# Block positions from a row's first edge and one count, instead of fifty counts over all edges

## What is computed

```python
h = relu(layernorm(x)); x = x + attention_layer(h, node_type, src, dst)   # L0
h = relu(layernorm(x)); x = x + degree_normalised_sum(h, src, dst)        # L1
h = relu(layernorm(x)); x = x + gated_sum(h, edge_attr, src, dst)         # L2
h = relu(layernorm(x)); x = x + mean_layer(h, src, dst)                   # L3
# each: out[n] = sum over the edges e with dst[e] == n of f(h[src[e]], ...)
```

## Time and profile before

| | us |
|---|---|
| median of 3 runs | 5079.63 (5073.73 to 5083.69) |
| the profiled execution | 5077.58 |
| its span | 5075.4 |
| busy: POOL / VectorE / TensorE / ScalarE | 3396.0 / 3117.0 / 3020.8 / 1527.4 |
| mean granted TensorE clock | 0.717 of full |

### The profile page before, as it was taken

How to read it: one execution, slowest core, us unless ns; L and a number is a source line. 1 busy time by engine, 2 the same in 40 slices (tenths; PEclk the granted TensorE clock), 3 DMA queues, 4 the chain that set the end, 5 groups by cost and what they waited for, 6 DMA issues and landing times.

```text
span 5075.4 us, 78070 instructions
## 1 busy us (share of the span) xinstructions
PE 3020.8 (60%) x15683; PEld 2534.0 (50%) x15684; DVE 3117.0 (61%) x8273; ACT 1527.4 (30%) x2888; POOL 3396.0 (67%) x3564
## 2 busy tenths in 40 slices
PE   1846555555563444455555999999996444444443
PEld 1535455545553444444443777777775343434433
DVE  6467777777788666645553677777775344444443
ACT  3223333333313000001111666666664122222222
POOL 1277777777600777777774777777774777777775
PEclk9957777877777555557776999999998555555555
DMA  2367877877831222222224767767776222222224
GB/s 51 83 178 215 231 230 225 225 227 226 215 92 34 53 53 52 53 59 66 65 66 49 197 186 188 186 185 189 186 186 118 53 56 56 56 56 55 56 56 41
DMA packets 536532, 616.06 MB, mean 121 GB/s; under 512 B 98004, under 2 KB 420607, under 8 KB 536352
## 3 DMA queue, kind: packets, MB, share of 16 engines
q0 software_dynamic: 142176, 349.02, 27.2%
q1 hardware_dynamic: 394176, 265.13, 19.5%
HBM read 529.54 MB, written 84.25 MB: 121 GB/s over the span
## 4 chain that ended last, share of the span: by engine, by line
POOL 43%; issue 20%; DMA 14%; DVE 10%; PE 7%; DVEq 2%; ACT 2%; SPq 1%; POOLq 0%; ACTq 0%
POOL G L658 43%; DMA G<-tab,SRC 9%; DMA mvd<-G 3%; DVE ACCR L1384 3%; PE PB L493 2%; PE PSA L876 2%; PE PB L1066 1%; DVEq L617 1%; DMA MV<-mvd 1%; DVE ACCR L1856 1%; PE PB L486 1%; PE PB L1004 0%; DVE FLG L1838 0%; PE PB L1058 0%; ACT PB L1230 0%
## 5 line engine op out<-in xcount | busy, mean ns | idle before, releaser
L658 POOL DMA_INDIRECT G<-tab,SRC x3520 | 3358.2, 954 | 1432.9 <-issue 1044.5
L1384 DVE TENSOR_TENSOR ACCR<-ACCR,PSA 128x128 f32 (+2 forms) x3536 | 1127.7, 319 | 748.8 <-PE PSA L876 389.8
L876 PE MATMUL PSA<-G,S 128*128 128x128 f32 x3520 | 857.3, 420 | 1157.7 <-DMA G<-tab,SRC 975.8
L876 PEld LDWEIGHTS PSA<-G,S 128*128 128x128 f32 x3520 | 736.0, 309 | 1267.9 <-DVE ACCR L1384 690.9
L1367 DVE TENSOR_TENSOR S<-PB,REL 128x512 f32<-128x512 f32 x884 | 606.3, 686 | 38.9 <-DVE MASK L1436 13.7
L1004 PE MATMUL PB<-QTR,ST 128*128 x1792 | 339.8, 350 | 301.4 <-ACT ST L1193 147.4
L1004 PEld LDWEIGHTS PB<-QTR,ST 128*128 128x128 f32 x1792 | 299.9, 253 | 336.1 <-issue 335.7
L876 PE MATMUL PSA<-FLG,S 128*128 128x256 f32 x1760 | 427.2, 387 | 2.8 <-DVE FLG L1838 2.6
L876 PEld LDWEIGHTS PSA<-FLG,S 128*128 128x128 f32 x1760 | 340.5, 194 | 149.3 <-issue 88.3
L876 PE MATMUL PSA<-SCR,S 128*128 128x137 f32 x1792 | 332.0, 343 | 17.8 <-DVE ACCR L1384 17.6
L876 PEld LDWEIGHTS PSA<-SCR,S 128*128 128x128 f32 x1792 | 307.9, 249 | 22.8 <-DVE SCR L1747 22.8
(11 more groups left out here) (313 smaller groups left out, 3748.1 us busy)
## 6 DMA issues: line engine op xcount, KB each, us to landing
mvd<-G SPq DMA_DIRECT2D x224, 256.0 KB
MV<-mvd SPq DMA_DIRECT2D x224, 256.0 KB
G<-tab,SRC POOLq DMA_INDIRECT x3520, 2.5
SCR<-in_ea_t SPq DMA_DIRECT2D x880, 64.0 KB
S<-relt SPq DMA_DIRECT2D x224, 128.0 KB, 4.9
SCR<-reld SPq DMA_DIRECT2D x220, 128.0 KB
tab<-SCR SPq DMA_DIRECT2D x57, 128.0 KB, 1.8
tab<-G SPq DMA_DIRECT2D x50, 128.0 KB, 1.7
```

Of the source, the lines that this page charges most:

```text
L658: nc.gpsimd.indirect_dma_start(out=rows[:, slot, j, :], out_offset=None, in_=table, in_offset=bass.IndirectOffsetOnAxis(ap=SRC[:, k:k + 1] ...
L876: last = nc.tensor.matmul((PSA if banks is None else banks)[:, par, j, 0:width], S[:, slot, j, :], rhs(j), start=True, stop=True)
L1384: v_.tensor_tensor(rows, rows, banks[:, par, j, 0:width], ALU.add).then_inc(s["rows_added"], 1)
```

## The change

The 50 counts over all edges go, on VectorE and on ScalarE, with their thresholds. In their place each of 128 partitions finds the position for its own threshold, 128p (only those of partitions 0 to 49 are used):

1. SyncE loads the first edge's destination of each of the 128 rows, one word each, instead of the array.
2. VectorE puts these 128 words on a diagonal, TensorE spreads them to all partitions with a matmul of ones, and VectorE counts on partition p how many are under 128p. That number less one (not below 0) is the only row in which the stretch can begin.
3. POOL fetches that row for each partition with one indirect transfer: 128 rows of 831 words.
4. VectorE makes one count over 831 columns, adds 831 times the row number, puts the 50 results on a diagonal, and the same matmul as before (L956 there) brings them to all partitions.

```diff
+            pool.wait_ge(row_known, 1)
+            nc.gpsimd.indirect_dma_start(
+                out=DSTI, out_offset=None, in_=a["dst_pm"],
+                in_offset=bass.IndirectOffsetOnAxis(ap=row_i[:, 0:1], axis=0)).then_inc(dst_loaded, 16)
...
-            sp.dma_start(DSTI, a["dst_pm"]).then_inc(dst_loaded, 16)
+            with nc.allow_non_contiguous_dma(reason="a column"):
+                sp.dma_start(FIRSTI, a["dst_pm"][:, 0:1]).then_inc(firsts_loaded, 16)
...
-            pe.wait_ge(counted, half + 1)
-            pe.wait_ge(counted_too, NE - half)
+            pe.wait_ge(firsts_put, 1)
+            nc.tensor.matmul(FIRSTP, ones, FIRSTD, start=True, stop=True).then_inc(firsts_spread, 1)
+            pe.wait_ge(counted, 1)
             nc.tensor.matmul(PB[0][:, 0:NE], ones, cnt, start=True, stop=True).then_inc(reckoned, 1)
...
-            act.wait_ge(counted, 1)
-            def count(b):
-                nc.scalar.activation(JUNKA, DSTF, ACT.Sign, bias=thr_half[:, bass.ds(b, 1)], scale=-1.0,
-                                     accum_out=cnt[:, bass.ds(b, 1)]).then_inc(counted_too, 1)
-            count(half)
-            with act.Fori(half + 1, NE) as b:
-                act.wait_ge(counted_too, b - half)
-                count(b)
...
-            c(v_.tensor_copy(thr, thrI))
-            c(v_.tensor_scalar(thr_half, thr, -0.5, None, ALU.add))
...
-            c(v_.memset(cnt, 0.0))
+            c(v_.tensor_scalar(edge_f, minus_p, -float(P), None, ALU.mult))
             c(v_.memset(cum, 0.0))
+
+            dve.wait_ge(firsts_loaded, 16)
+            c(v_.tensor_copy(count_f, FIRSTI))
+            v_.tensor_scalar(FIRSTD, ident[:, :], count_f, None, ALU.mult).then_inc(firsts_put, 1)
+            dve.wait_ge(firsts_spread, 1)
+            c(v_.tensor_scalar(JUNK[:, 0:P], FIRSTP, edge_f, 0.0, ALU.is_lt, ALU.add, accum_out=row_f))
+            c(v_.tensor_scalar(row_f, row_f, -1.0, 0.0, ALU.add, ALU.max))
+            c(v_.tensor_copy(row_i, row_f))
+            dve.sem_inc(row_known, 1)
+
             dve.wait_ge(dst_loaded, 16)
-            v_.tensor_copy(DSTF, DSTI).then_inc(counted, 1)
-            with dve.Fori(0, half) as b:
-                dve.wait_ge(counted, b + 1)
-                v_.tensor_scalar(JUNK, DSTF, thr[:, bass.ds(b, 1)], 0.0, ALU.is_lt, ALU.add,
-                                 accum_out=cnt[:, bass.ds(b, 1)]).then_inc(counted, 1)
+            c(v_.tensor_copy(DSTF, DSTI))
+            c(v_.tensor_scalar(JUNK, DSTF, edge_f, 0.0, ALU.is_lt, ALU.add, accum_out=count_f))
+            c(v_.scalar_tensor_tensor(count_f, row_f, float(TC), count_f, ALU.mult, ALU.add))
+            v_.tensor_scalar(cnt, ident[:, 0:NE], count_f, None, ALU.mult).then_inc(counted, 1)
             dve.wait_ge(reckoned, TOTALS)
-            c(v_.tensor_copy(bf[:, 0:half], PB[0][:, 0:half]))
-
-            c(v_.tensor_scalar(bf[:, half:NE], PB[0][:, half:NE], 0.5, float(P * TC) / 2, ALU.mult, ALU.add))
+            c(v_.tensor_copy(bf, PB[0][:, 0:NE]))
```

More of the change, by code:

```diff
@@ L340, in build @@
         c_ready = sem("consts_ready")
-        dst_loaded = sem("dst_loaded")
+        firsts_loaded = sem("first_edges_loaded")
+        firsts_put, firsts_spread = sem("first_edges_put"), sem("first_edges_spread")
+        row_known = sem("boundary_row_known")
+        dst_loaded = sem("boundary_row_loaded")
         x_loaded = sem("x_loaded")
@@ L344, in build @@
         counted = sem("counted")
-        counted_too = sem("counted_too")
         planned = sem("planned")
@@ L396, in build @@
         JUNK = SCR[:, 2 * T:2 * T + TC]
-        JUNKA = G[:, 2 * T:2 * T + TC]
+        FIRSTI = G[:, 2 * T:2 * T + 1].bitcast(I32)
+        FIRSTD = G[:, 2 * T + P:2 * T + 2 * P]
+        FIRSTP = PB[1][:, 0:P]
         VAL = SCR[:, 2 * T:3 * T].rearrange("p (c e) -> p c e", c=NC)
@@ L413, in build @@
         WEIGHT = ACCR[:, accw + NS * HEADS:accw + NS * HEADS * (1 + TYPES)].rearrange("p (b t h) -> p b t h", t=TYPES, h=HEADS)
-        half = NE // 2
-        thr_half = cut(NE)
-        thr, cnt, bf, b16f, tiles_f, zer, cum, rel0, delta = (cut(NE) for _ in range(9))
+        row_f, row_i, edge_f, count_f = cut(1), cut(1, I32), cut(1), cut(1)
+        cnt, bf, b16f, tiles_f, zer, cum, rel0, delta = (cut(NE) for _ in range(8))
         bi = cut(NE, I32)
@@ L429, in build @@
         MD = cut(NC * NE).rearrange("p (c b) -> p c b", c=NC)
-        thrI = cut(NE, I32)
         iotaI = cut(P, I32)
@@ L669, in _ @@
             nc.gpsimd.iota(iotaI, pattern=[[1, P]], base=0, channel_multiplier=0)
-            nc.gpsimd.iota(thrI, pattern=[[P, NE]], base=0, channel_multiplier=0)
             nc.gpsimd.iota(pI, pattern=[[0, 1]], base=0, channel_multiplier=1)
             nc.gpsimd.iota(cI, pattern=[[8, NC]], base=0, channel_multiplier=0).then_inc(c_ready, 1)
+            pool.wait_ge(row_known, 1)
+            nc.gpsimd.indirect_dma_start(
+                out=DSTI, out_offset=None, in_=a["dst_pm"],
+                in_offset=bass.IndirectOffsetOnAxis(ap=row_i[:, 0:1], axis=0)).then_inc(dst_loaded, 16)
             pool.wait_ge(planned, WINDOWS_KNOWN)
```

## The result

The changed kernel takes **5054.32 us** (median, 5049.21 to 5060.48), the kernel before 5079.63 (5073.73 to 5084.35): ratio **0.9952, 95% interval 0.9937 to 0.9966**. That is a gain of 24 us by the ratio, between 17 and 32. The forecast, 5059.4 us with a gain of 20.2, lies in that interval, and the range 5050 to 5070 holds the result. The profiled execution took 5054.32 us with a span of 5051.9.

The account below looks back on a forecast made before the run. POOL bounds the kernel, its first edge gather (240.14 us) delayed by the setup's counts. Block positions at 17.96 instead of 38.19 us gain 20.2 one for one: 5079.63 - 20.2 = 5059.4 us, range 5050 to 5070.

Parts of the forecast that it names:

- The single words: Setup's load of the 128 rows' first destinations: 3.4 us, bounds 3.4 and 10.0, landing at 4.14.
- Spreading and counting the firsts: Setup, ones-matmul 1.03 us, count over 128 columns 0.45, two one-column steps of 0.19: from 4.71 to 6.57.
- The semaphore to POOL: Setup, from VectorE's last small step to POOL's indirect gather: 1.02 us, so the gather starts at 7.59.
- The transfer: POOL's indirect gather of 128 rows, 415.5 KB: 6.7 us, landed at 14.29; lower end 3.7, upper end landing at 18.5.
- the fair share of the bandwidth: Gather beside the x load: half of 285 GB/s makes 2.9 us of its bytes, 5.6 with 2.7.
- the repeated row: Gather: 79 of 128 partitions read row 127; at the broadcast loads' price 4.0 us over 2.7, 6.7 in all.
- The rival of the starved gather: Gather waits till the DMA engines are free, lands at 18.5: gain 16.0, 5063.6 us; chance 0.20.
- Behind the transfer: Setup, from landing to block positions (cast, count, combining, diagonal, matmul, copy): 3.67 us, positions at 17.96 against 38.19.
- Later needs: Planner's weights land at 23.0, PE needs them at 23.5; x landed by 18, its statistics start at 41.8: nothing late.
- the gain is eaten: Projection: shifted bursts meet TensorE's low clock, five more blocks cost 10 us, 5069.6, no change; chance 0.08.
- The loop in instruction memory: VectorE or ScalarE loop body crosses one block more, refetched each pass: 68 us, 5127, slower; chance 0.04.
- The slow words: Setup's single-word load takes 9.3 us instead of 3.4: gain 14.3, 5065.3 us; chance 0.08.

Follow-up runs that it names:

- the candidate: Changed kernel with all loads behind the indirect transfer and only the 50 used rows: 5041.82 us against 5067.69 before, ratio 0.9950; slower chip 6369.43, ratio 0.9973.

## Why the prediction was right, step by step

**The bound and the way to it: right.** The counts mattered only through the first edge gather. Doses of 18 us (twice), 21 and 24 to 26 us at the first gather were found again at the end to some 5 us between the medians, though that of the candidate on the slower chip (24.8 us, with an interval of 11 to 24) lies just outside its interval. I had the way right, and my sum of the steps came out 0.8 us off, partly by luck, as the following shows.

**The single words:** forecast 3.4 us, measured 1.7 (landed at 2.4). VectorE didn't wait at all, its clearing ended at 3.54 and the cast started at 3.57, 0.6 before my 4.18. So the 0.6 us isn't what the faster load was worth. It comes from the small steps on thresholds, which I had counted at nothing because VectorE waits for a transfer behind them. It didn't do that before either: the array had landed at 3.9 us, and the last clearing ended at 4.10.

```profile
4.00 0.10 DVE L1472 MEMSET QTR<- 128x50 f32 x1
```

The row I chose for the load, 64 words, was one among heavy traffic; mine went first.

```profile
G<-in_dst_pm SPq DMA_DIRECT2D x1, 0.5 KB, 1.7
...
G<-in_dst_pm,QTR POOLq DMA_INDIRECT x1, 7.9
```

**Spreading and counting the firsts:** from 4.71 to 6.57 by the sum, from 4.05 to 5.67 in the trace, 1.62 for 1.86. **The semaphore to POOL:** 1.02 forecast, 0.36 measured (5.67 to 6.03). The row I took from the plan has 0.90 in the profile after as well (31.48 to 32.38), so it is the price of that place, where POOL passes a wait and raises a semaphore ahead of the gather, and not of any wait. The transfer was thus issued at 6.03 and not 7.59.

**The transfer:** 6.7 us forecast, 7.9 measured, and for a wrong reason. Both of my grounds failed: the fair share of the bandwidth (once it ran, POOL's queue took the larger part, 0.43 MB against 0.26 in 2 us) and the repeated row. The time until the first packet was 5.5 us, 3.8 more than alone, and for these 3.8 my sum had nothing. The number was near by luck, because the 4.0 us that I gave the repeated row happened to be about as large. What it is short by lies in the bytes: alone they took 4.0 us, where I had started from 2.7. Two details of that step: half of 285 GB/s makes 3.0 us of these bytes and not 2.9, which changes nothing, and the 0.5 us for POOL's slower path at the lower end had no row; through POOL's queue the same bytes took 4.0 us alone, against 3.2 for the array's load. The rival of the starved gather was nearer in mechanism, since the transfer did stand behind x for 3.8 us, but not in size: it landed at 13.95, before my 14.29, and not at 18.5. The Trainium skill's rule that the engines go round robin between queues ("DMA: Bandwidth & Descriptors", section "Queues, rings and completion order") agrees with the stretch in which both queues moved packets, 60.2% to 41.9% from 11.5 to 13.5 us. The fair share from the start, which the prediction read out of it, didn't come: the rule speaks of queues that have work, and no view shows whether POOL's had any in the 5.5 us before.

**Behind the transfer:** 3.67 forecast, 3.20 measured (13.95 to 17.15). I had taken 2.11 from cast to next step out of the loop of rows 2; without a loop it was 1.75. In sum 17.15 for 17.96, the errors being -0.6, -0.2, -0.7, +1.2 and -0.5.

**Later needs:** PE was just in time within 0.2 us of the forecast (23.66 for 23.5), x in time with 24 us to spare (landed at 16.9, first read at 40.85). **The projection** took 0.8 us back in this pair of traces, by a store it waited for, and nothing in the pair on the slower chip. My rival "the gain is eaten" had it by the granted clock. The clock did cost what it had cost before and no more, a first group of 4.05 us after the idle stretch (granted clock 0.50 from 107 to 111 us) and 2.10 two blocks on (1.00 from 115 to 119):

```profile
109.20 4.05 PE L495 MATMUL PB<-W,G 128*128 128x384 f32 x6
...
116.05 2.10 PE L495 MATMUL PB<-W,G 128*128 128x384 f32 x6
```

**The loop in instruction memory** didn't happen: over the whole execution the instruction queues carried 53 and 128 packets, 53 and 127 before. **The slow words** are refuted by the 1.7 us.

**The 5 us of difference** between forecast and median aren't a failed step. 20.07 us stand at the first edge gather. The rest is layer 0's 5.0 less 1.5 behind it in one pair of traces; on the slower chip layer 0 of the same pair is 1.0 us longer, not shorter, and it alone scatters by more. On the faster kind its cause stays open.

## What to carry to other kernels

Ask of a setup step when the first instruction of the pacing engine starts, and price the step by that alone; then check that by putting the time back as idle work, which here showed the one for one to some 4 us (16.7 for 17.7 and 21.4 for 17.9). A dependent small load in a setup should be issued and landed before the bulk loads are asked for: it is the backlog of the other queue that it pays for, 3.8 us here, whether it is large or small. What that order is worth at the end of this kernel the timings don't resolve. And take a transfer's price from a row with the same traffic beside it, not from the row most like it in shape.

## What the runs showed of the hardware

A transfer of POOL's queue issued into a full SyncE queue moved no packet for 5.5 us, with small loads beside it for 3.0, and alone for 1.7. Beside the full queue the 5.5 didn't depend on its size (166 or 415.5 KB), nor on 79 partitions reading one row. A VectorE count took 1.29 us in a loop of one instruction and 1.12 written out.

The kernel before took 5.07 and 5.08 ms on two chips and 6.32 and 6.39 ms on two others. The first edge gather comes at the same time to 0.6 us in three programs that ran on both kinds, and to 2.1 us in the fourth. On the slower kind the edge passes are longer, with VectorE idle before its row additions; first the changed kernel on the faster kind, then on the slower (busy us, mean ns, idle us and its releasers):

```profile
L1384 DVE TENSOR_TENSOR ACCR<-ACCR,PSA 128x128 f32 (+2 forms) x3536 | 1126.0, 318 | 740.6 <-PE PSA L883 381.5
```

```profile
L1384 DVE TENSOR_TENSOR ACCR<-ACCR,PSA 128x128 f32 (+2 forms) x3536 | 1130.3, 320 | 1695.1 <-remote 683.6 <-issue 652.7 <-PE PSA L883 64.9
```

The additions themselves are as fast. What grew is idle time put down to issue and to "remote", a releaser that the profile can't name. In the program, these additions are the instructions before which VectorE loads the block's number from a row into a register, but no run tried that, so the cause isn't shown.
